# Attention and mixture-of-experts layer: the work between the two phases is placed anew, ten record loads change queue, and the second weights are loaded one expert at a time

## The chip, the cores and the metric

The kernel runs on one core of a Trainium2 chip. The engines of the core run programs of their own and meet by semaphores: TensorE (PE in the profile) multiplies matrices, VectorE (DVE), ScalarE (ACT) and GpSimd (POOL) work elementwise, SyncE (SP) issues transfers. The metric is the device time of one execution in microseconds (us). Before the change it was 968.32 us in the median of three runs (965.58 to 971.52).

## What is computed

32 blocks of 128 tokens with 256 features. First cross-attention with 16 heads and an unusual score, then a feed-forward layer with 8 experts, of which each token takes 2:

```python
x = x + attention(layernorm(x), ctx) @ Wo + bo
# feed-forward: t tokens, 8 experts, H = 1024
logits = einsum('btd,de->bte', layernorm(x), Wr)
w, idx = top_k(softmax(logits), 2);  w = w / sum(w)
h = gelu(einsum('btd,edh->ebth', x, W1) + b1)
y = einsum('ebth,ehd->ebtd', h, W2) + b2
out = x + einsum('ebtd,bte->btd', y, dispatch)
```

## The kernel before

The first phase walks over 16 pairs of token blocks (`NP` = 16). In it attention is computed, the tokens are routed, and each token's normalised features, its shares and its number are written as a record of 265 words into the table `xrec` in HBM, at a row of its expert (`scatter`, indirect DMAs of GpSimd). On the side the weights are turned into two halves of float16; the first weights stay in SBUF (`w1s`), the second go to HBM (`w2s`) by `store_w2`.

The second phase takes 71 slots (`NSLOT`) of 128 records, all of one expert each. Slot s has these steps:

- `load_records(s)`: SP loads 128 records into `rb`, of which there are ten (`U`). Slot s + 10 can be loaded when `add(s)` has landed.
- `turn_records(s)` on TensorE turns them, `take_records(s)` on VectorE copies them to `xt`.
- `first_product(s)`: 48 matmuls on TensorE into one of two pairs of banks. The weights of the expert are at an address in a register, since the expert of a slot is known at run time only (`expert_of` loads it).
- `gelu(s)` on ScalarE, eight activations; `split_hidden(s)` on VectorE makes two halves of float16.
- `second_product(s)`: 24 matmuls on TensorE.
- `weigh(s)` on VectorE: scale, bias, share; into one of two `yw`.
- `add(s)` on GpSimd: an indirect DMA that adds the 128 rows to `out`. It waits for the landing of `add(s-1)`.

Each engine's program is written out by hand in order. In the loop over s, TensorE runs turn(s+3), first(s+2), second(s); ScalarE runs gelu(s); VectorE runs take(s+3), split(s+2), weigh(s). TensorE's turn(s+1) waits for take(s), because there is one bank for it; `weigh(s)` waits for the landing of `add(s-2)`, because there are two `yw`.

The first twenty slots (`SOON`) are laid out from the counts of the first 24 blocks, so that the second phase can begin before the last pairs are routed. The rest of the work for the last pair (`project_out`, `heads_back`, `turn_on`, `residual`, `turn_y`, `record_high`, `record_low`, `logits`, `choose`, `counts`, `ranks`, `shares`, `positions`, `scatter`, `last_tables`) is interleaved with the first slots. `last_tables` lays out slots 20 to 70. `record_low(b)` on GpSimd waits for `record_high(b)` on ScalarE; both halves stand in GpSimd's program ahead of `add(0)`.

On SP, the lines around the change are: load records 0 to 8, store the last of the second weights, load all eight experts' second weights (`w2s_sb`, 1 MB each) behind one another without a wait, tell TensorE expert by expert that they are there (`w2_ready`), and load records 9 to 19.

## Time and profile before

| | |
|---|---|
| median of three runs | 968.32 us |
| the profiled execution | 970.74 us |
| its span, first to last instruction | 968.9 us |
| mean granted TensorE clock | 0.977 of full |
| PE busy | 898.1 us (93%) |
| DVE busy | 697.2 us (72%) |
| ACT busy | 634.5 us (65%) |
| POOL busy | 415.5 us (43%) |

The times of the rows are microseconds from the start of the span. A timeline row gives start, length, engine, line, operation, output and inputs, the number of instructions merged into it, and in brackets how long the engine was idle before it and which instruction ended that. "issue" means that the profile shows nothing that was waited for.

### The profile page before, as it was taken

To read this page: it belongs to the slowest core of one execution; us is meant where nothing else is said; L and a number is where in the kernel's file an instruction comes from. 1 tells how busy PE (TensorE), PEld (TensorE's weight loads), DVE (VectorE), ACT (ScalarE), POOL (GpSimd) and SP (SyncE) were. 2 spreads that over 40 slices of the span, in tenths; PEclk is the share of its full clock that TensorE was granted. 3 is DMA by queue.
4 is the path that set the end of the run, shared out by engine and by line. 5 is a ranking of instruction groups with operands and counts; after the bars stand their busy time and mean duration, and the time that the engine had idled before them with its cause. 6 is when DMAs were issued, how large, how long until landed. Compare 5 with 4: busy or idle time off the path is not lost.

```text
span 968.9 us, 30634 instructions
## 1 busy us (share of the span) xinstructions
PE 898.1 (93%) x10701; PEld 789.8 (82%) x10701; DVE 697.2 (72%) x1833; ACT 634.5 (65%) x1236; POOL 415.5 (43%) x540
## 2 busy tenths in 40 slices
PE   3999999998999999989899699899999999999994
PEld 2788887787877877878777589799999999999993
DVE  7677888777987887779768577766666666666662
ACT  3688887787877877878857356455555455554551
POOL 6344456538546565385253532623222232222322
PEclk9799999999999999999979799999999999999998
DMA  5222122314132333253044773443333233332222
GB/s 150 70 72 89 41 83 80 112 41 128 57 99 76 126 123 103 92 171 111 20 139 134 275 273 52 85 93 52 51 52 51 47 52 52 52 51 48 46 30 22
DMA packets 61892, 84.82 MB, mean 88 GB/s; under 512 B 9872, under 2 KB 55312, under 8 KB 59568
## 3 DMA queue, kind: packets, MB, share of 16 engines
q1 hardware_dynamic: 47504, 64.26, 21.0%
q0 software_dynamic: 13296, 18.00, 11.1%
q8 instruction: 91, 1.49, 0.6%
q10 hardware_dynamic: 944, 0.60, 0.2%
q14 instruction: 57, 0.47, 0.2%
HBM read 49.86 MB, written 31.92 MB: 84 GB/s over the span
## 4 chain that ended last, share of the span: by engine, by line
PE 74%; issue 7%; DVE 6%; ACT 6%; POOL 3%; another core or an unknown queue 1%; DMA 1%; DVEq 0%; POOLq 0%; ACTq 0%
PE s_ps L711 10%; PE u_ps L711 10%; PE pv_ps L729 9%; PE gen L729 9%; PE gen L502 5%; PE gen L495 5%; PE s_ps L485 5%; PE u_ps L473 3%; PE pv_ps L519 2%; PE gen L544 2%; ACT pt L827 2%; PE gen L415 2%; PE gen L680 2%; PE gen L418 2%; PE gen L422 1%
## 5 line engine op out<-in xcount | busy, mean ns | idle before, releaser
L1567 POOL DMA_INDIRECT out<-yw,rb x71 | 110.3, 1553 | 269.4 <-DVE yw L1392 253.4
L928 ACT ACTIVATE h<-s_ps,b1t,inv 128x128 f32<-128x128 f32 x288 | 107.8, 457 | 89.6 <-PE s_ps L711 79.3
L928 ACT ACTIVATE h<-u_ps,b1t,inv 128x128 f32<-128x128 f32 x280 | 104.7, 459 | 87.4 <-PE u_ps L711 86.4
L1375 DVE TENSOR_SCALAR hs<-h,hsc 128x512 f16<-128x512 f32 x142 | 69.7, 491 | 120.4 <-ACT h L928 102.0
L827 ACT ACTIVATE pt<-gen,escale 128x512 f32<-128x512 f32 x128 | 86.8, 686 | 50.4 <-PE gen L502 34.5
L1377 DVE SCALAR_TENSOR_TENSOR hs<-h,hsc,hs 128x512 f16<-128x512 f32 x142 | 106.7, 751 | 5.1
L711 PE MATMUL s_ps<-xt,w1s 128*128 128x128 f16 x1728 | 104.8, 220 | 2.2 <-issue 2.2
L1517 POOL DMA_INDIRECT xrec<-rec,idx x64 | 77.8, 1215 | 60.9 <-DVE idx L1229 44.7
L711 PE MATMUL u_ps<-xt,w1s 128*128 128x128 f16 x1680 | 102.5, 220 | 0.9 <-issue 0.9
L711 PEld LDWEIGHTS s_ps<-xt,w1s 128*128 x1728 | 99.8, 99 | 2.8 <-issue 2.3
L729 PE MATMUL pv_ps<-w2s_sb,hs 128*128 x864 | 100.5, 272 | 0.5 <-issue 0.5
L711 PEld LDWEIGHTS u_ps<-xt,w1s 128*128 x1680 | 97.2, 99 | 2.0 <-issue 1.5
L1124 DVE SCALAR_TENSOR_TENSOR tw<-th,s_ps 128x1024 f32<-128x1024 f32 x64 | 77.9, 1217 | 27.2 <-PE s_ps L485 21.9
L729 PE MATMUL gen<-w2s_sb,hs 128*128 x840 | 97.4, 273 | 0.0
L729 PEld LDWEIGHTS pv_ps<-w2s_sb,hs 128*128 128x128 f16 x864 | 82.5, 98 | 11.0 <-issue 1.5
L495 PE MATMUL gen<-idf,tw 128*128 128x128 f32 x512 | 79.5, 278 | 10.7 <-DVE wcl L1283 7.9
L502 PE MATMUL gen<-negb,mhl 128*128 128x128 bf16 x1024 | 79.2, 220 | 9.7 <-POOL mhl L1488 9.3
L729 PEld LDWEIGHTS gen<-w2s_sb,hs 128*128 128x128 f16 x840 | 80.9, 98 | 8.8
L1130 DVE TENSOR_REDUCE tm<-tw 128x8 f32<-128x1024 f32 x64 | 78.1, 1220 | 2.2
L817 ACT ACTIVATE th<-u_ps 128x1024 f32<-128x1024 f32 x64 | 65.6, 1026 | 20.5 <-PE u_ps L473 20.3
L502 PEld LDWEIGHTS gen<-negb,mhl 128*128 128x128 bf16 x1024 | 67.9, 99 | 13.6 <-POOL mhl L1488 11.6
L485 PE MATMUL s_ps<-kt,qt 32*128 32x128 f32 x1024 | 75.6, 286 | 0.9 <-DVE tw L1124 0.9
(251 smaller groups left out, 1741.8 us busy)
## 6 DMA issues: line engine op xcount, KB each, us to landing
wl<-L_ffn_W SPq DMA_DIRECT2D x16, 1024.0 KB
rb<-xrec SPq DMA_DIRECT2D x71, 132.5 KB
w2s<-wst SPq DMA_DIRECT2D x8, 1024.0 KB
w2s_sb<-w2s SPq DMA_DIRECT2D x8, 1024.0 KB, 20.4
xin<-x SPq DMA_DIRECT2D x32, 128.0 KB, 3.5
cin<-ctx SPq DMA_DIRECT2D x32, 128.0 KB, 2.1
xres<-x SPq DMA_DIRECT2D x32, 128.0 KB
out<-x SPq DMA_DIRECT2D x30, 128.0 KB, 2.0
```

Source lines behind the costliest of these rows:

```text
L485: ins = pe.matmul(s_ps[:, i, j * P:(j + 1) * P], qt[b][rws, j // 2, :], kt[b][rws, j // 2, j % 2, :], start=True, stop=True)
L495: pe.matmul(g[:, j * P:(j + 1) * P], tw[h][:, i, j, :], idf[:, :], is_transpose=True, start=(j == 0), stop=False)
L502: ins = pe.matmul(g[:, j * P:(j + 1) * P], m, negb[:, :], start=False, stop=(j == 3 and part == 1))
L711: ins = pe.matmul(hbank[n % HBANKS][:, o:o + SLOT], w, xt[s % 2][:, xp, k, :], start=(t == 0), stop=(t == len(terms) - 1))
L729: ins = pe.matmul(y, hs[s % 3][:, hp, m, :], w, start=(m == 0 and t == 0), stop=(m == HC - 1 and t == 2))
L827: act.activation(pt[n % 2][:, i, :], turn(f"ex{n}{i}", p)[:, :], ACT.Exp, scale=escale[:, :]).then_inc(sig(f"ex{n}{i}"), 1)
L928: ins = act.activation(h32[n % HBANKS][:, m % HB, :], hbank[n % HBANKS][:, o:o + SLOT], ACT.Gelu, scale=inv1[:, bass.ds(ex, 1)].bitcast(F3 ...
L1124: dve.scalar_tensor_tensor(tw[h][:, :, :, :].rearrange("p i j k -> p (i j k)"), th[h][:, :], -1.0, s_ps[:, :, :].rearrange("p i k -> p (i ...
L1130: dve.tensor_reduce(tm[h][:, :], tw[h][:, :, :, :].rearrange("p i j k -> p (i j) k"), AX.X, ALU.max).then_inc(sig(f"tm{n}"), 1)
L1377: dve.scalar_tensor_tensor(lo, h, scale, hi, ALU.mult, ALU.subtract).then_inc(sig("lo"), 1)
L1517: pool.indirect_dma_start(xrec_d[:, :], bass.IndirectOffsetOnAxis(ap=idx[:, i, t:t + 1], axis=0), rec[m % 2][:, t, :], None).then_inc(sig( ...
L1567: pool.indirect_dma_start(out[:, :], bass.IndirectOffsetOnAxis(ap=rb[j][:, D + NE:D + NE + 1], axis=0), yw[s % 2][:, :], None, compute_op= ...
```

## The change

**SP.** `b2s`, now placed first in the memory of the second phase, is loaded ahead of the records. Ten record loads follow instead of nine, then the second weights: each expert's load begins when the one before has landed. The store of the last second weights comes ahead of expert 2, and a wait for all stores ahead of expert 5. Records 10 to 19 are no longer loaded by SP.

**GpSimd.** It loads records 10 to 19 itself, each between the landing of `add(s-1)` and the issue of `add(s)`, s from 1 to 10. The scatters of the last pair move from slots 5 to 8 to slots 9 to 12.

**TensorE, ScalarE, VectorE.** The first slots begin ahead of the rest of the last pair, and that work is spread over later slots. Addresses for `first_product` are computed ahead for the first slots too. ScalarE loads its gelu table before the first slot. VectorE's `weight_low` of the last pair and most of the scale steps (`hidden_scales`, without `inv1`) come later. From slot 60 on (`SHORT`) TensorE runs first(s+1), second(s).

```diff
+    gelu_one = alloc(ctx, "gelu_one", [P, 1], F32)
...
+            for b in range(2):
+                sp.wait_ge(*at(f"v{b}", NP))
+            sp.dma_start(b2s[:, :, :], b2.partition_broadcast(P)).then_inc(sig("ldb2"), 16)
             sp.wait_ge(*at("soon", 1))
             sp.wait_ge(*dma("scat", 4 * (SOON_PAIR + 1)))
-            for b in range(2):
-                sp.wait_ge(*at(f"v{b}", NP))
-            for s in range(U - 1):
+            for s in range(U):
                 load_records(s)
-            store_w2(NP - 1)
             sp.wait_ge(*at("pv3", NP))
-            for e in range(NE - 1):
+            for e in range(NE):
+                if e == 2:
+                    store_w2(NP - 1)
+                if e == W2_SOON:
+                    sp.wait_ge(*dma("stw", NE))
                 load_w2(e)
-                if e == 0:
-                    sp.dma_start(b2s[:, :, :], b2.partition_broadcast(P)).then_inc(sig("ldb2"), 16)
-            sp.wait_ge(*dma("stw", NE))
-            load_w2(NE - 1)
-            for e in range(NE):
                 sp.wait_ge(*dma(f"ldw2_{e}", 1))
                 sp.sem_inc(sig("w2_ready"), 1)
-            for s in range(U - 1, SOON):
-                load_records(s)
...
-                pe.wait_ge(*dma(f"ldrec{s % U}", s // U + 1))
+                if U <= s < SOON:
+                    pe.wait_ge(*dma(f"ldsoon{s % 5}", 1 if s < U + 5 else 2))
+                else:
+                    pe.wait_ge(*dma(f"ldrec{s % U}", s // U if s >= SOON else 1))
...
-            def first_product(s, ex):
+            def first_product(s, ex, ahead=()):
...
+                        for address in itertools.islice(ahead, 2 * DC):
+                            pe.to_reg(address)
...
+            experts = [expert_of(pe, 0)]
+            for address in first_addresses(experts[0]):
+                pe.to_reg(address)
+            turn_records(0)
             project_out(0, NP - 1)
+            experts.append(expert_of(pe, 1))
+            turn_records(1)
+            first_product(0, experts[0], first_addresses(experts[1]))
             heads_back(1, NP - 1)
-            for s in range(3):
-                turn_records(s)
-            experts = [expert_of(pe, s) for s in range(3)]
-            first_product(0, experts[0])
+            turn_records(2)
+            experts.append(expert_of(pe, 2))
+            first_product(1, experts[1], first_addresses(experts[2]))
             turn_on(1, NP - 1)
-            first_product(1, experts[1])
-            project_out(1, NP - 1)
-            turn_y(0, NP - 1)
             for s in range(NSLOT):
                 if s + 3 < NSLOT:
                     turn_records(s + 3)
-                if s + 2 < NSLOT:
-                    first_product(s + 2, experts[2])
+                if s + 2 < SHORT:
+                    first_product(s + 2, experts[2], second_addresses(experts[0]) if s == 0 else ())
+                elif SHORT - 2 < s < NSLOT - 1:
+                    first_product(s + 1, experts[1], second_addresses(experts[0]))
                 if s == 0:
+                    project_out(1, NP - 1)
+                if s == 1:
+                    turn_y(0, NP - 1)
+                if s == 2:
                     logits(0, NP - 1)
+                if s == 3:
                     turn_y(1, NP - 1)
-                if s == 1:
+                if s == 4:
                     logits(1, NP - 1)
-                if s == 4:
+                if s == 7:
                     ranks(NP - 1)
                 if s + 3 < NSLOT:
                     experts.append(expert_of(pe, s + 3))
-                later = second_addresses(experts[1]) if s + 1 < NSLOT else ()
-                second_product(s, experts[0], itertools.chain(later, first_addresses(experts[3]) if s + 3 < NSLOT else ()))
+                if s + 3 < SHORT:
+                    ahead = itertools.chain(second_addresses(experts[1]), first_addresses(experts[3]))
+                elif s + 3 == SHORT:
+                    ahead = second_addresses(experts[1])
+                elif s + 2 < NSLOT:
+                    ahead = first_addresses(experts[2])
+                else:
+                    ahead = ()
+                second_product(s, experts[0], ahead)
...
+            act.activation(gelu_one[:, :], mhalf[:, :], ACT.Gelu)
...
-                    act.wait_ge(*at("scales", 1))
+                    act.wait_ge(*at("inv1", 1))
...
             for s in range(NSLOT):
                 gelu(s)
-                if s == 0:
+                if s == 1:
                     o_turned(1, NP - 1)
-                if s == 1:
+                if s == 2:
                     store_x1(0, NP - 1)
                     record_high(0, NP - 1)
-                if s == 2:
+                if s == 5:
+                    store_x1(1, NP - 1)
                     record_high(1, NP - 1)
-                    store_x1(1, NP - 1)
-                if s == 5:
+                if s == 7:
                     route_exp(NP - 1)
...
-                if 0 <= it - 1 < NP:
+                if 0 <= it - 1 < NP - 1:
...
+            take_records(0)
+            dve.tensor_scalar(inv1[:, :], k1[:, :], 25.0, float(ONE), ALU.subtract, ALU.mult).then_inc(sig("inv1"), 1)
+            take_records(1)
+            hidden_scales()
+            experts = [expert_of(dve, s) for s in range(2)]
             residual(0, NP - 1)
-            heads_back(1, NP - 1)
-            take_records(0)
-            take_records(1)
-            experts = [expert_of(dve, s) for s in range(2)]
             split_hidden(0, experts[0])
             take_records(2)
-            residual(1, NP - 1)
+            heads_back(1, NP - 1)
             split_hidden(1, experts[1])
             for s in range(NSLOT):
                 if s + 3 < NSLOT:
                     take_records(s + 3)
-                if s == 0:
-                    logits(0, NP - 1)
                 if s + 2 < NSLOT:
                     experts.append(expert_of(dve, s + 2))
+                if s + 2 < SHORT:
                     split_hidden(s + 2, experts[2])
+                elif SHORT - 2 < s < NSLOT - 1:
+                    split_hidden(s + 1, experts[1])
+                if s == 0:
+                    weight_low(NP - 1)
                 if s == 1:
+                    residual(1, NP - 1)
+                if s == 2:
+                    logits(0, NP - 1)
+                if s == 4:
                     logits(1, NP - 1)
                 weigh(s, experts[0])
                 experts.pop(0)
-                if s == 1:
+                if s == 5:
                     choose(NP - 1)
-                if s == 2:
+                if s == 6:
                     counts(NP - 1)
-                if s == 5:
+                if s == 8:
                     shares(NP - 1)
-                if s == 6:
+                if s == 9:
                     positions(NP - 1)
-                if s == 7:
+                if s == 10:
                     last_tables()
...
+            def load_records(s):
+                j = s % U
+                if s >= U + 5:
+                    pool.wait_ge(*dma(f"ldsoon{s % 5}", 1))
+                row = pool.value_load(slot_row[0:1, s:s + 1], min_val=0, max_val=NE * REGION)
+                pool.dma_start(rb[j][:, :], xrec_d[bass.ds(row, SLOT), :]).then_inc(sig(f"ldsoon{s % 5}"), 16)
...
                 if s:
                     pool.wait_ge(*dma(f"add{(s - 1) % U}", (s - 1) // U + 1))
+                    if s - 1 + U < SOON:
+                        load_records(s - 1 + U)
...
-                if 5 <= s < 9:
+                if 9 <= s < 13:
                     for i in range(2):
-                        scatter(s - 5, i, NP - 1)
+                        scatter(s - 9, i, NP - 1)
...
+    W2_SOON = 5
+    SHORT = 60
...
+        b2s = alloc(f, "b2s", [P, NE, D], F32)
```

`hidden_scales` holds the eight scale steps that stood ahead of the second phase, without the one for `inv1`.

Three places show how rows move. The first is TensorE at the start of the second phase, before (L541 and L544 are `project_out`, L680 `turn_records`, L269 `expert_of`, L711 `first_product`):

```order
L541 MATMUL gen<-bop,ones_b 128x256 [waits act_exp]
L544 MATMUL gen<-wo_sb,ot 128x256 [waits ote]
L544 MATMUL gen<-wo_sb,ot 128x256
L527 MATMUL gen<-idf,osb 128x128 [waits osb,ote]
L527 MATMUL gen<-idf,osb 128x128 x3
L680 MATMUL gen<-id,rb 128x128 [waits dve_route,ldrec0]
L680 MATMUL gen<-id,rb 128x128 x3
...
L269 TENSOR_LOAD slot_e
L269 ISA x2
L711 ISA [waits dve_max,xte]
L711 MATMUL s_ps<-xt,w1s 128x128 x2
L711 REGISTER_ALU
```

and now (L681 is `turn_records`, L270 `expert_of`, L740 the addresses ahead, L712 and L715 `first_product` with the addresses of the next slot):

```order
L270 TENSOR_LOAD slot_e [waits soon]
L270 ISA x2
L740 ISA x6
L681 MATMUL gen<-id,rb 128x128 [waits dve_route,ldrec0]
L681 MATMUL gen<-id,rb 128x128 x3
L539 MATMUL gen<-bop,ones_b 128x256 [waits act_exp]
L542 MATMUL gen<-wo_sb,ot 128x256 [waits ote]
...
L712 MATMUL s_ps<-xt,w1s 128x128 [waits dve_max,xte]
L712 MATMUL s_ps<-xt,w1s 128x128 x5
L715 ISA
L712 MATMUL s_ps<-xt,w1s 128x128 x6
```

The turn of slot 0 stands ahead of `project_out`, and the register instruction that stood before nearly every matmul has become one group for each six.

The second place is ScalarE. Before, the record's high half of block 1 (L847) and the store (L935) stood behind the gelu of slot 2:

```order
L928 ISA
L928 ACTIVATE h_1<-s_ps,b1t,inv 128x128
L847 ACTIVATE rec<-xn 128x256 [waits y1,scat]
L851 ACTIVATE xn2t<-gen 128x256 [waits lg,xu1]
L935 DMA out<-x 128x256 [waits dve_second1]
L269 TENSOR_LOAD slot_e
L269 ISA x2
```

Now they stand behind the gelu of slot 5 (L952), L959 being the store and L868 the high half:

```order
L952 ISA
L952 ACTIVATE h_3<-u_ps,b1t,inv 128x128
L959 DMA out<-x 128x256 [waits dve_second1]
L868 ACTIVATE rec<-xn 128x256 [waits y1,scat]
L872 ACTIVATE xn2t<-gen 128x256 [waits lg,xu1]
L270 TENSOR_LOAD slot_e
L270 ISA x2
```

The third is GpSimd behind the two `record_low`, before:

```order
L1493 TENSOR_TENSOR rec<-xn,rec 128x256 [waits rh0]
L1493 TENSOR_TENSOR rec<-xn,rec 128x256 [waits rh1]
L1567 DMA out<-yw,rb 4224x256 [waits stx1,stx0,yw]
L1567 DMA out<-yw,rb 4224x256 [waits add0,yw]
L1567 DMA out<-yw,rb 4224x256 [waits add1,yw]
```

and now (L1607 is `add`, L1591 and L1592 `load_records`):

```order
L1524 TENSOR_TENSOR rec<-xn,rec 128x256 [waits rh0]
L1524 TENSOR_TENSOR rec<-xn,rec 128x256 [waits rh1]
L1607 DMA out<-yw,rb 4224x256 [waits stx1,stx0,yw]
L1591 TENSOR_LOAD slot_row [waits add0,yw]
L1591 ISA x2
L1592 ISA
L1592 DMA rb<-xrec 128x265
L1607 DMA out<-yw,rb 4224x256
L1591 TENSOR_LOAD slot_row [waits add1,yw]
```

A register load and a plain DMA have come between one add and the next.

## Rows read from the trace of the kernel before

**Rows 1.** Windows view: stretch, its length, busy us (instructions) by engine, clock, DMA.
```profile
core 0: us, PE busy (x) PEld busy (x) DVE busy (x) ACT busy (x) POOL busy (x), PEclk, DMA share, GB/s
616.00:621.00 5.00, 4.09 (x47) 3.53 (x45) 3.67 (x8) 1.97 (x6) 2.66 (x3) 0.70 0.53 113
624.00:900.00 276.00, 276.00 (x3801) 262.43 (x3800) 177.52 (x350) 150.14 (x400) 78.09 (x51) 1.00 0.33 55
```

**Rows 2.** Timeline of TensorE at the start of the second phase.
```profile
538.44 0.28 PE L541 MATMUL gen<-bop,ones_b 96*128 96x256 bf16 x1
...
539.86 0.39 PE L680 MATMUL gen<-id,rb 128*128 128x128 f16 x4
546.74 0.59 PE L680 MATMUL gen<-id,rb 128*128 128x128 f16 x4 [6.50 <-DVE xt L1362]
...
550.51 4.10 PE L711 MATMUL s_ps<-xt,w1s 128*128 128x128 f16 x48 [1.99 <-issue]
...
554.74 3.94 PE L711 MATMUL u_ps<-xt,w1s 128*128 128x128 f16 x48
```

**Rows 3.** Timeline of TensorE, slots 7 and 12 and 13.
```profile
585.52 0.39 PE L680 MATMUL gen<-id,rb 128*128 128x128 f16 x4
585.75 2.84 PE L711 MATMUL s_ps<-xt,w1s 128*128 128x128 f16 x48
...
615.69 0.38 PE L680 MATMUL gen<-id,rb 128*128 128x128 f16 x4 [1.93 <-DVE xt L1362]
...
624.04 0.39 PE L680 MATMUL gen<-id,rb 128*128 128x128 f16 x4
```

**Rows 4.** Timeline of VectorE.
```profile
538.72 2.35 DVE L1277 SCALAR_TENSOR_TENSOR wst<-wl,wsc,wst 128x2048 f16<-128x2048 f32 x1
540.98 0.16 DVE L960 TENSOR_SCALAR kb<-b1ss 128x8 int32<-128x8 int32 x1
...
544.28 0.42 DVE L1154 TENSOR_TENSOR x<-gen,xres 128x256 f32<-128x256 f32 x1
...
545.49 0.25 DVE L1137 RECIPROCAL rz<-gen 128x16 f32<-128x16 f32 x1
...
556.40 0.49 DVE L1375 TENSOR_SCALAR hs<-h,hsc 128x512 f16<-128x512 f32 x1 [8.62 <-ACT h L928]
...
558.87 0.41 DVE L1362 COPY xt<-gen 128x512 f16<-128x512 f16 x1
...
568.82 0.48 DVE L1386 SCALAR_TENSOR_TENSOR yb<-pv_ps,inv,b2s 128x256 f32<-128x256 f32 x1 [0.92 <-PE pv_ps L729]
...
569.73 0.42 DVE L1362 COPY xt<-gen 128x512 f16<-128x512 f16 x1
...
608.75 0.48 DVE L1386 SCALAR_TENSOR_TENSOR yb<-gen,inv,b2s 128x256 f32<-128x256 f32 x1
```

**Rows 5.** Timeline of ScalarE.
```profile
565.01 0.35 ACTq L935 DMA_DIRECT2D out<-x  x1
565.30 0.43 ACT L847 ACTIVATE rec<-xn 128x256 f16<-128x256 f32 x1
...
576.37 2.90 ACT L928 ACTIVATE h<-s_ps,b1t,inv 128x128 f32<-128x128 f32 x8 [3.03 <-issue]
```

**Rows 6.** Timeline of GpSimd: a scatter, a low half, the last three adds.
```profile
542.35 0.96 POOL L1517 DMA_INDIRECT xrec<-rec,idx  x1 [0.31 <-issue]
...
565.81 1.02 POOL L1493 TENSOR_TENSOR rec<-xn,rec 128x256 f16<-128x256 f32 x1 [1.61 <-DMA out<-x]
...
951.83 1.55 POOL L1567 DMA_INDIRECT out<-yw,rb  x1 [3.92 <-DVE yw L1392]
956.94 1.54 POOL L1567 DMA_INDIRECT out<-yw,rb  x1 [3.56 <-DVE yw L1392]
961.44 1.55 POOL L1567 DMA_INDIRECT out<-yw,rb  x1 [2.95 <-DMA out<-yw,rb]
```

**Rows 7.** SP's timeline with the record loads; landing of the eight loads of L363.
```profile
528.31 9.58 SPq L360 DMA_DIRECT2D rb<-xrec  x9
...
DMA to landing us min/median/max: 14.2/20.4/26.4
```

18 lines of the change are left out of this document (8 added, 10 removed).

## Prediction

> **What bounds the kernel now.** I read the windows view first. From 624 to 900 us TensorE is busy all the time at full clock, 3801 matmuls, and one slot has 76 of them (4 turns of the records, 48 of `first_product`, 24 of `second_product`), so a slot takes 276 / 50 = 5.52 us [rows 1]. I write turn(s), fp(s), sp(s), take(s), split(s), weigh(s), add(s) for the steps of slot s. The change leaves those matmuls alone; only where TensorE stands still can it gain or lose. The timeline of TensorE shows three such places. At the entry TensorE ends the attention work at about 540.3, waits 6.50 us for VectorE's `xt`, then 1.99 us for nothing but its own sequencer ("issue"), and starts fp(0) at 550.51 [rows 2]. Around 615 turn(12) waits 1.93 us for `last_tables`, and from turn(12) to turn(13) 8.35 us pass instead of 5.52 [rows 3], with a granted clock of 0.70 from 616 to 621 [rows 1]. At the end three adds follow one another on GpSimd at 951.83, 956.94 and 961.44, each held by the landing of the last: 5.1 and 4.5 us apart [rows 6].
>
> Times below are on the clock of the trace of before; LAND(s) is the landing of add(s).
>
> **Entry, a gain.** `weight_low` leaves the path (2.35 us [rows 4]), most of the scale steps come behind take(1), and addresses are computed ahead: fp(1) took 3.94 us for what 2.84 us do later, at a full clock, with a register instruction before most of its matmuls; that is 1.1 us for each of three slots [rows 2, 3]. Worked through: values end at 538.4; one value load costs 1.99 / 3 = 0.66, and I give the eight register rows 0.5: turn(0) at 539.6. take(0), `project_out(0)` (with `heads_back` 1.4 us in the trace, I take 1.0) and a second value load put fp(0) at 541.8, its end at 544.5. VectorE: take(1) by 542.3; scales 540.98 to 544.28 are 3.3 us, less 0.7 for `inv1`, now ahead: 544.9; two value loads 1.3; `residual(0)` 1.2; split(0) 2.5 (556.40 to 558.87): 549.9, take(2) 550.3, `heads_back` 0.7 [rows 4]. TensorE's `turn_on` waits for that: fp(2) at 551.5. From here a slot is 5.5 plus what stands between: `project_out(1)` 1.0, `turn_y` 0.3, `logits` 0.5. fp(5) starts at 569.9, and TensorE would be free for turn(7) at 575.5. Before it came at 585.52 [rows 3]: 10.0 us ahead. The gelu table load runs beside idle time. Bounds: 1 us earlier if the value loads cost half, 3 later if ScalarE's wait in `record_high(0)` for `turn_y(0)` reaches TensorE.
>
> **The hold, a new wait.** `record_high(1)` now stands behind gelu(5). GpSimd has `record_low(1)`, which needs it, ahead of add(0); weigh(2) waits for LAND(0); and behind weigh(2) on VectorE is take(6), for which turn(7) waits. gelu(5) ends at 569.9 + 1.35 (half of fp) + 0.2 + 2.90 = 574.4; DMA issue and copy 0.72 [rows 5]; `record_low` 1.02; add(0) starts at 576.3; landing seen 4.6 later (between 4.5 and 5.1 [rows 6]): LAND(0) = 580.9. weigh and take are 1.4, so turn(7) comes at 582.3: 6.8 us lost of the 10.0, and 3.2 left. Before, nobody waits there.
>
> **The chain of adds.** Records 10 to 19 leave SP's queue for GpSimd's, each between LAND(s-1) and add(s), for s = 1 to 10. SP needs 9.58 us for nine such loads, (9.58 - 0.34) / 8 = 1.155 apart, of which 0.34 is the DMA instruction: 0.8 for the value load and registers [rows 7]. GpSimd's DMA issue is nearest to the scatter's 0.96; the add's 1.55 and SP's 0.34 are the ends [rows 6, 7]. So an add takes 4.5 + 0.8 + 0.96 = 6.3 us in this stretch; from below 4.5 + 0.8 + 0.34 = 5.6, from above 5.1 + 0.8 + 1.55 + 0.3 = 7.75. That is more than 5.52, and the hold has used up the slack: weigh(s) waits for LAND(s-2). LAND(8) = 580.9 + 8 x 6.3 = 631.3. `choose`, `counts` and `ranks`, now at slots 5 to 7, fit into the 0.8 us per slot that TensorE gets back as idle time, with the chain still ahead at slot 10.
>
> Behind weigh(10) stands `last_tables`. In the trace from the start of such a weigh to the turn are 615.69 - 608.75 = 6.9 us [rows 3, 4]. So turn(15) comes at 638.2. Before it is at 624.04 + 2 x 5.52 = 635.1. Loss 3.1. TensorE has then been idle about 6 us (1.93 us ahead of the low clock in the trace); I charge the same 8.35 - 5.52 = 2.8 us again [rows 3], between 0 and 4.
>
> The Trainium skill ("DMA: Bandwidth & Descriptors", "Latency and other measured facts") gives a floor of about 600 ns for `tensor_load`; SP's 0.8 us agrees with it. By the same page, "Issuing engine by pattern", a plain load belongs on SP; it gives about 1 us to the first byte from GpSimd and 0.6 us from SP. With only 0.6 + 0.96 the chain would have a period of 6.1 us and the time would be 1.9 us lower. No row here shows a plain load from GpSimd.
>
> **Other loads.** `load_w2(0)` is issued at about 539.6, behind ten record loads at 1.155 us and `b2s`, and sp(0) comes at 555. Before, a megabyte among nine took 14.2 to 26.4 us [rows 7]; even 14.2 is enough, and alone it should be less. Expert 2's load waits behind `weight_low` (about 560), but experts come in order, some six slots each (the 24 blocks counted by then give 24 x 128 x 2 / 8 = 768 rows to each of eight), so nobody asks for it before 590. Cost 0. Slots from 20 on need the eight late scatters (behind adds 9 to 12, done about 655); turn(20) is past 665: 10 us of cover, cost 0.
>
> **Tail.** From slot 60 the first product runs one slot ahead instead of two. sp(68) moves ahead of fp(70), 2.7 us, so add(68) is at 949.1, add(69) 5.1 later, add(70) at 958.7 instead of 961.44: gain 2.7. TensorE's own end does not move. Between 0 and 2.9.
>
> **Sum.** 3.1 + 2.8 - 2.7 = 3.2 us slower. The profiled execution lasted 970.74 us, its span 968.9; the median of the three runs is 968.32, 2.4 below it. On the median: **971.5 us**. About 1% is what a measurement of this kernel can tell from no change, so I forecast no change.
>
> **The rivals.**
> - *Slower: the load's cost on GpSimd is that of an add.* With 1.55 us of descriptor work and some of the load's packets before the add's, the period is 7.6: 971.5 + 8 x 1.3 = 982 us. It decides (over 978) from a period of 7.1. For it: this is the same queue, and GpSimd's indirect DMAs take 0.96 to 1.55. Against: a plain load has no index per row. 0.22.
> - *The load is cheap,* period 5.6: 971.5 - 8 x 0.7 = 966 us. For it: SP's 0.34. Against: no DMA of GpSimd's in the trace is under 0.96. 0.16.
> - *Faster: the hold is not paid.* If add(0) lands while VectorE is busy anyway, 6.8 us come back; without the hold the adds have some 5 us of slack, so with a cheap load the chain (another 5.6 us) and 3 us of the bubble at turn(15) go too: about 956 us. One of them alone is not 1%. Against it stands the row order of three engines. 0.13.
> - *Another wait at the entry* (`turn_y(0)`, the second weights) takes 3 to 6 us more than I charged; since the chain starts from it, all of it stays: 975 to 978. 0.09.
> - *The forecast,* 968 to 977 with periods between 5.9 and 7.0: 0.40, the largest share.
>
> **Range and chances.** From 963, where half of the hold and a cheap load meet, to 982, the slow rival. Faster by over 1% (under 958.6): 0.13; within 1%: 0.63; slower by over 1% (over 978.0): 0.24.
>
> **What would show each step.** fp(0) near 542 and no "issue" wait before it (entry). The first add of GpSimd some 2 us behind the end of gelu(5), and TensorE idle 6 to 7 us before turn(7), released by `xt` (hold). Adds 1 to 10 spaced 6.3 us, with a VectorE wait for "DMA out" before `yw` (chain). A gap of 5 to 6 us before turn(15) with a granted clock near one half behind it (`last_tables`). The last add 2.7 us closer to TensorE's end (tail). I am wrong if the first add is issued before 570, if adds 1 to 10 keep 5.5 us, or if TensorE waits for `w2_ready`.

## The result, and the profile after the change

The changed kernel takes 985.88 us in the median of four runs (983.95 to 987.14), the kernel before 967.91 us in four runs that include one beside it. The ratio is 1.0181, with a 95% interval of 1.0144 to 1.0217. It is slower by 1.8%, where 971.5 us and no change were forecast, and above the range's upper end of 982.

| | before | after |
|---|---|---|
| median | 967.91 us | 985.88 us |
| the profiled execution | 970.74 us | 986.65 us |
| its span | 968.9 us | 985.0 us |
| mean granted clock | 0.977 | 0.969 |
| the last attention matmul ends | 538.4 us | 536.2 us |
| from there to turn(7) | 47.1 us | 53.8 us |
| from there to turn(17) | 107.7 us | 125.9 us |
| from turn(17) to the span's end | 322.8 us | 322.9 us |

The end of the last attention matmul differs from profile to profile (533.4 to 539.1 us in those on chips of this speed), so I count from there. The whole loss, 18.2 us, lies between it and turn(17). Behind turn(17) nothing is lost and nothing won.

TensorE's timeline of the changed kernel (start us, us, engine, line, operation, output and inputs, count, and the idle time before it with what ended it):

```profile
535.33 0.94 PE L517 MATMUL pv_ps<-pt,vz 128*32 128x128 f32 x16
...
539.14 2.84 PE L712 MATMUL s_ps<-xt,w1s 128*128 128x128 f16 x48
...
549.78 0.66 PE L532 MATMUL gen<-idf,on 128*128 128x128 f32 x2 [3.54 <-DVE on L1166]
...
550.66 4.82 PE L712 MATMUL s_ps<-xt,w1s 128*128 128x128 f16 x48
...
568.32 4.50 PE L732 MATMUL gen<-w2s_sb,hs 128*128 x24 [6.11 <-SPq L381]
...
590.04 0.59 PE L681 MATMUL gen<-id,rb 128*128 128x128 f16 x4 [5.54 <-DVE xt L1376]
590.42 5.33 PE L712 MATMUL s_ps<-xt,w1s 128*128 128x128 f16 x48
...
619.88 0.19 PE L562 MATMUL gen<-hot,lstrict 128*128 128x32 bf16 x1 [3.23 <-DVE acc_cnt L1216]
...
620.74 5.28 PE L732 MATMUL gen<-w2s_sb,hs 128*128 x24 [0.64 <-issue]
```

There are four waits of over 3 us, and behind each the next product runs for 4.5 to 5.3 us: 4.82 and 5.33 for a first product that takes 2.84 undisturbed, 4.50 and 5.28 for a second product that takes 2.78. It pays another 1.7 to 2.5 us. The waits are at `turn_on` (before fp(2)), at sp(1), at turn(7), and at the ranks before sp(7). A shorter wait, 2.06 us at turn(10), is followed by a first product of 4.47 us. The first and the third wait were forecast with what is waited for, `heads_back` and the hold; the second and the fourth were not, and of the low clock behind any of the four nothing was charged.

GpSimd's timeline of the changed kernel, from the release of the first add:

```profile
583.97 0.64 POOL L1524 TENSOR_TENSOR rec<-xn,rec 128x256 f16<-128x256 f32 x1 [12.26 <-ACT rec L868]
584.77 1.67 POOL L1607 DMA_INDIRECT out<-yw,rb  x1 [0.17 <-issue]
590.62 0.63 POOL L1592 DMA_DIRECT2D rb<-xrec  x1 [4.18 <-issue]
591.56 1.72 POOL L1607 DMA_INDIRECT out<-yw,rb  x1 [0.30 <-issue]
596.81 0.60 POOL L1592 DMA_DIRECT2D rb<-xrec  x1 [3.53 <-DVE yw L1406]
597.72 1.62 POOL L1607 DMA_INDIRECT out<-yw,rb  x1 [0.30 <-issue]
```

This is the hold and the chain: the first add leaves 1.3 us behind the ScalarE copy of 583.46 that it was held for, and add(1) to add(10) stand 6.22 us apart in the mean (591.56 to 647.55 in nine steps, the single ones 5.92 to 7.10).

### The profile page after: what moved, and what is told of

It reads as the page before. It is cut to its first block, busy times and chain, and to the rows that moved or that the text cites. A ratio compares the mean times of both kernels' runs of the same rounds, so it can differ in the third digit from the quotient of the medians.

```text
span 985.0 us, 30587 instructions
## 1 busy us (share of the span) xinstructions
PE 904.3 (92%) x10701; PEld 795.3 (81%) x10701; DVE 693.9 (70%) x1833; ACT 633.6 (64%) x1237; POOL 420.5 (43%) x550
## 4 chain that ended last, share of the span: by engine, by line
PE 69%; issue 10%; ACT 6%; DVE 5%; POOL 4%; DMA 2%; another core or an unknown queue 1%; POOLq 0%; ACTq 0%; DVEq 0%
PE gen L732 9%; PE s_ps L712 8%; PE pv_ps L732 8%; PE u_ps L712 8%; PE gen L500 5%; PE gen L493 5%; PE s_ps L483 5%; PE u_ps L471 2%; PE pv_ps L517 2%; PE gen L542 2%; ACT pt L848 2%; DMA out<-yw,rb 2%; PE gen L413 2%; PE gen L416 2%; PE gen L681 1%
## 5 line engine op out<-in xcount | busy, mean ns | idle before, releaser
L1607 POOL DMA_INDIRECT out<-yw,rb x71 | 110.5, 1557 | 230.3 <-DVE yw L1406 211.6
L952 ACT ACTIVATE h<-s_ps,b1t,inv 128x128 f32<-128x128 f32 x288 | 106.6, 461 | 111.2 <-PE s_ps L712 110.6
L952 ACT ACTIVATE h<-u_ps,b1t,inv 128x128 f32<-128x128 f32 x280 | 104.3, 461 | 91.3 <-PE u_ps L712 88.5
L732 PE MATMUL gen<-w2s_sb,hs 128*128 x840 | 102.0, 280 | 7.2 <-SPq L381 6.1
L712 PE MATMUL s_ps<-xt,w1s 128*128 128x128 f16 x1728 | 107.1, 224 | 0.2 <-issue 0.2
L712 PEld LDWEIGHTS s_ps<-xt,w1s 128*128 x1728 | 102.7, 101 | 0.3 <-issue 0.3
L712 PE MATMUL u_ps<-xt,w1s 128*128 128x128 f16 x1680 | 101.5, 221 | 0.6 <-issue 0.6
L712 PEld LDWEIGHTS u_ps<-xt,w1s 128*128 x1680 | 97.0, 99 | 0.9 <-issue 0.9
```

The source lines that it names most:

```text
L712: ins = pe.matmul(hbank[n % HBANKS][:, o:o + SLOT], w, xt[s % 2][:, xp, k, :], start=(t == 0), stop=(t == len(terms) - 1))
L732: ins = pe.matmul(y, hs[s % 3][:, hp, m, :], w, start=(m == 0 and t == 0), stop=(m == HC - 1 and t == 2))
L952: ins = act.activation(h32[n % HBANKS][:, m % HB, :], hbank[n % HBANKS][:, o:o + SLOT], ACT.Gelu, scale=inv1[:, bass.ds(ex, 1)].bitcast(F3 ...
L1607: pool.indirect_dma_start(out[:, :], bass.IndirectOffsetOnAxis(ap=rb[j][:, D + NE:D + NE + 1], axis=0), yw[s % 2][:, :], None, compute_op= ...
```

## The experiments

All times count from the end of the last attention matmul of the kernel's own profile. "To the end" is the span less that point. The ratio is to the kernel before, run beside it.

| kernel | median us | ratio [95%] | turn(7) | turn(17) | to the end |
|---|---|---|---|---|---|
| before | 967.91 | 1 | 47.1 | 107.7 | 430.5 |
| after | 985.88 | 1.0181 [1.0144, 1.0217] | 53.8 | 125.9 | 448.8 |
| r1_residual | 983.59 | 1.0172 [1.0137, 1.0207] | 49.7 | 120.4 | 443.5 |
| r2_store5 | 984.21 | 1.0190 [1.0154, 1.0225] | 52.2 | 123.1 | 446.4 |
| r3_hold | 980.48 | 1.0135 [1.0100, 1.0170] | 48.1 | 118.0 | 440.4 |
| r4_sploads | 983.33 | 1.0177 [1.0140, 1.0214] | 53.0 | 121.6 | 443.9 |
| t1_ranks | 981.91 | 1.0154 [1.0137, 1.0172] | 53.7 | 120.0 | 443.4 |
| t2_four | 965.79 | 0.9987 [0.9970, 1.0004] | 41.1 | 105.5 | 427.5 |
| t4_pool_loads | 970.65 | 1.0007 [0.9980, 1.0034] | 40.8 | 109.9 | 435.1 |
| t5_all | 961.43 | 0.9914 [0.9880, 0.9948] | 40.8 | 99.4 | 421.6 |
| t6_all_entry | 959.13 | 0.9896 [0.9874, 0.9919] | 40.6 | 99.3 | 421.9 |
| d1_residual_late | 966.37 | 1.0003 [0.9980, 1.0025] | 47.9 | 106.1 | 428.2 |
| d2_hold_back | 966.39 | 0.9998 [0.9980, 1.0015] | 46.2 | 106.3 | 428.2 |
| d3_ranks_early | 967.04 | 0.9990 [0.9973, 1.0007] | 41.0 | 106.5 | 428.3 |
| d4_loads_gpsimd | 970.55 | 1.0032 [1.0006, 1.0058] | 41.1 | 106.9 | 430.2 |
| s3_before_short | 964.71 | 0.9982 [0.9964, 1.0000] | 47.2 | 105.9 | 426.1 |
| s4_before_serial | 967.08 | 1.0001 [0.9987, 1.0015] | 47.6 | 105.3 | 427.7 |

Two more ran beside each other on a faster chip, where the kernel before takes 956.34 us: d5_serial_w2 955.19 us, 0.9988 [0.9967, 1.0009], and t7_all_again (t5_all once more) 948.03 us, 0.9922 [0.9896, 0.9949]. Their turn(17) comes at 104.4 and 98.5. The kernels of the table ran on several chips, on which the kernel before took 966.19 to 969.32 us, so between kernels the ratios compare better than the medians.

### One repair at a time

**The residual ahead of split(3).** The profile names a SyncE semaphore, L381, for the wait of sp(1); but slot 1 is of expert 0, whose weights sp(0) had used 12 us before. What stands directly ahead of it in time is VectorE:

```profile
565.32 0.49 DVE L1389 TENSOR_SCALAR hs<-h,hsc 128x512 f16<-128x512 f32 x1 [3.37 <-ACT h L952]
...
567.13 0.75 DVE L1391 SCALAR_TENSOR_TENSOR hs<-h,hsc,hs 128x512 f16<-128x512 f32 x1
567.80 0.42 DVE L1178 TENSOR_TENSOR x<-gen,xres 128x256 f32<-128x256 f32 x1
```

The last row is `residual(1)`. It reads the bank of `project_out(1)`, which is sp(1)'s result bank, and it ends at 568.22; sp(1) starts at 568.32. The change put it behind split(3), which waits for gelu(3), and gelu(3) stands on ScalarE behind `record_high(0)`, whose copy waited 4.81 us for `turn_y(0)`:

```profile
562.25 0.38 ACT L872 ACTIVATE xn2t<-gen 128x256 f32<-128x256 f32 x1 [4.81 <-PE gen L549]
563.67 2.90 ACT L952 ACTIVATE h<-u_ps,b1t,inv 128x128 f32<-128x128 f32 x8 [1.04 <-issue]
```

```diff
+                if s == 1:
+                    residual(1, NP - 1)
                 if s + 2 < SHORT:
                     split_hidden(s + 2, experts[2])
...
-                if s == 1:
-                    residual(1, NP - 1)
```

> The changed kernel with one step moved: VectorE's residual of the last block stands ahead of split(3), not behind it. Theory (the bank): sp(1) writes the bank that the output projection of the last block filled, and waits 6.1 us for VectorE to read it there; the gap before sp(1) goes (568.3 to about 562) and with it the 1.7 us that sp(1) ran slower at the low clock; both stay, since the chain of adds starts from gelu(5): 985.9 less 7 to 8, about 978. Rival (the second weights, which the profile names as what ended that wait): sp(1) still waits 6 us, 985.9 unchanged.

The wait of sp(1) shrank to 0.75 us and turn(6) stands at 35.2 instead of 42.4:

```profile
565.46 2.78 PE L732 MATMUL gen<-w2s_sb,hs 128*128 x24 [0.75 <-issue]
```

But turn(7) came only at 49.7: TensorE waited 8.55 us there for VectorE, which waited 12.5 us for the landing of an add. Of 7.2 us at turn(6), 5.5 were left at turn(17), and the median shows 2.3, where 7 to 8 were expected. The rival on the wait's cause has its own run:

```diff
-                if e == 2:
-                    store_w2(NP - 1)
                 if e == W2_SOON:
+                    store_w2(NP - 1)
                     sp.wait_ge(*dma("stw", NE))
```

> The changed kernel with the store of the last second weights put ahead of expert 5's load instead of expert 2's, so that the loads of experts 2 to 4 do not wait for VectorE's late half of those weights. Rival (sp(1) waits for second weights): they land at about 560, the wait of 6.1 us goes, about 978. Theory (the bank): sp(1) needs expert 0 only, the wait stays, 985.9 within 1.5 us.

The wait at sp(1) stayed, at 5.43 us, though SyncE had issued the loads of experts 0 to 4 by 558.1:

```profile
564.14 4.98 PE L731 MATMUL gen<-w2s_sb,hs 128*128 x24 [5.43 <-issue]
```

So it was not the second weights. In all three kernels sp(1) starts 0.10 us behind the end of `residual(1)`: 568.32 behind 568.22 in the changed kernel, 565.46 behind 565.36 in r1_residual, 564.14 behind 564.04 in r2_store5. The bank is shown by the pair of runs, and the name in the row was of a semaphore that had been met. The median of r2_store5 is 1.7 us lower and its ratio 0.09% higher, which tells nothing.

**The hold.** The high half of `record_high(1)` behind gelu(3); its second copy, now `copy_turned(1)`, stays behind gelu(5):

```diff
...
+                if s == 3:
+                    record_high(1, NP - 1)
                 if s == 5:
                     store_x1(1, NP - 1)
-                    record_high(1, NP - 1)
+                    copy_turned(1, NP - 1)
```

> The changed kernel with the high half of the last block's record made behind gelu(3); the store and the copy of the turned block stay behind gelu(5). Theory (the hold): GpSimd's low half runs at about 572, add(0) lands at 577 instead of 589, TensorE's wait of 5.5 us before turn(7) and the slow fp(6) (5.3 us for 2.8) go, and the adds are no longer behind: about 985.9 less 10, between 6 and 13. Rival (the late first add only uses slack, the entry sets the end): unchanged.

add(0) left at 574.61 and turn(7) waited for nothing. This is the largest gain of the single repairs: 7.9 us at turn(17), of which the median shows 5.4, just under the 6 to 13 expected.

**The record loads on SyncE again**, behind the second weights:

```diff
+            for s in range(U, SOON):
+                load_records(s)
...
-                    if s - 1 + U < SOON:
-                        load_records(s - 1 + U)
```

> The changed kernel with records 10 to 19 loaded by SP again, behind the second weights. The hold stays. Theory (the chain of adds): adds come 4.6 us apart until they have caught up, then 5.5 us, instead of 6.2; choose and ranks find VectorE in time; about 985.9 less 8, between 5 and 10. Rival (GpSimd's loads run inside waits that are there anyway): unchanged within 1.5 us.

The first six adds closed up to 4.92, 4.97, 5.59, 4.48 and 4.81 us. With the hold and the residual still in front, the time moved by 2.6 us in the median, 4.3 at turn(17): more than the rival's 1.5, less than the 5 to 10 of the theory.

**The ranks one slot later** on TensorE:

```diff
-                if s == 7:
+                if s == 8:
                     ranks(NP - 1)
```

> The changed kernel with ranks on TensorE one slot later (s == 8 for 7), nothing else. In all five traces with the new placement 13 us pass from turn(10) to turn(11) instead of 5.5: TensorE waits 3 to 5 us for VectorE's counts, which is late because ScalarE sat in route_exp, and then runs sp(7) at the low clock. Theory (several chains run side by side, so that one repair shows only down to the next): the wait and the low clock behind it go, but the adds of GpSimd, still 6.1 us apart since the late first one, hold turn(15) at about 111 us behind the attention's end instead of 114: 2 to 4 us faster than the changed kernel. Rival (the losses are independent and add): 8 us faster.

5.9 us less at turn(17), 4.0 in the median, the upper end of what the theory expected.

### Two parts put into the kernel before

```diff
-                if s + 2 < NSLOT:
+                if s + 2 < SHORT:
                     first_product(s + 2, experts[2])
+                elif SHORT - 2 < s < NSLOT - 1:
+                    first_product(s + 1, experts[1], second_addresses(experts[0]))
```

> The kernel before with only the end changed: from slot 60 first product one slot ahead instead of two, with its addresses. Prediction's term: the last add 2.7 us earlier, TensorE's own end where it was, so 965.5 for 968.2. Rival: the span's end does not follow the last add (behind the last add 9.9 us passed in the changed kernel, 7.5 before), so no gain.

```diff
-            for e in range(NE - 1):
+            for e in range(NE):
+                if e == NE - 1:
+                    sp.wait_ge(*dma("stw", NE))
                 load_w2(e)
...
+                sp.wait_ge(*dma(f"ldw2_{e}", 1))
+                sp.sem_inc(sig("w2_ready"), 1)
```

> The kernel before with only the second weights loaded one expert at a time, each at the landing of the last. Prediction's term: 0, within 1.5 us of before. Rival (TensorE waits for w2_ready, as the profile of the changed kernel names it): a wait of some us in front of sp(0) or sp(1), 3 to 6 us slower.

The first product one slot ahead from slot 60 (s3) brings a gain at the edge of what the times can show, 0.18% (interval 0 to 0.36%). The profile shows it plainly: the last add starts 3.91 us behind TensorE's end (955.24 behind 951.33) instead of 6.35 (961.44 behind 955.09), and from turn(17) to the end 320.2 us pass instead of 322.8. That is the tail's 2.7 us, within 0.1.

The second weights one by one (s4) cost nothing in the kernel before. Both profiles reach turn(17) 2 us earlier than that of the kernel before: from turn(12) to turn(13) 8.35 us pass in the profile on which the forecast rests, with a granted clock of 0.70 from 616 to 621, but 6.58 us in s3 and 5.64 in s4, with a clock of 1.00 there. So the 2.8 us that I took for the low clock is one execution's value.

### All together, and each put back

t2_four holds the four repairs (residual, hold, ranks, loads on SyncE):

> The changed kernel with four steps put right at once: residual of the last block ahead of split(3), its high half behind gelu(3), records 10 to 19 loaded by SP, ranks at slot 8. Theory: no chain is left to take over; turn(17) comes 102 to 105 us behind the attention's end instead of 125.9 (before: 107.7), and the tail keeps its 2.7 us: 15 to 22 us faster than the changed kernel and 0 to 1% faster than before. Rival (the repairs overlap with something not yet seen): not more than the 4.4 us that the hold alone gave, still over 1% slower than before.

It gives back 20 us in the median and 1.94% in the ratio. The single repairs (residual, hold, loads, ranks) gave 2.3, 5.4, 2.6 and 4.0 us in their medians, and only 0.09, 0.46, 0.04 and 0.27% in the ratios to the kernel before on their own chips, each uncertain by some 0.35%. A new wait stands at turn(10), because record 10 is now behind eight second weights loaded one after another:

```profile
600.76 0.40 PE L680 MATMUL gen<-id,rb 128*128 128x128 f16 x4 [4.10 <-DMA rb<-xrec]
```

Two ways around it. t4_pool_loads has t2_four's repairs but for that of the loads. Its expectation says that `choose` and `counts` move too; the edit moves `ranks` alone, as in t2_four:

> The changed kernel with three repairs: the residual of slot 1 stands ahead of split(3) on VectorE, the hold at turn(7) is gone, and choose, counts and ranks stand one slot later (ranks at slot 8). The records' loads stay on GpSimd. Theory: the record wait of 4.1 us that TensorE showed at turn(10) in t2_four is gone, since no record load stands behind a second-weights load on SyncE any more, but the adds stay 6.1 to 6.3 us apart and GpSimd's last DRAIN is 5.6 us where t2_four had 4.8: 962 to 966 us. Rival (the loads of records on GpSimd are the main cost): above 972 us.

> All of t4_pool_loads, and route_exp one slot later, the records of slots 10 to 19 on SyncE, and the second weights of experts 0 to 4 queued together ahead of the store, 5 to 7 one after another. Theory: no record waits behind a serial load, the waits at turn(10) to turn(12) are under 1 us, 958 to 963 us. Rival (the wait moves to another buffer at the same place): 964 to 968 us, as t2_four.

The theory of t4 missed: leaving the loads on GpSimd gave 970.65 us, 5 us over it and just under the rival. TensorE waits over 2 us at three turns instead of one, turn(9), turn(10) and turn(15), for a VectorE that had waited 5.61, 2.57 and 0.94 us for the landing of an add and then had its own work to do, at turn(10) that of `choose` and at turn(15) that of `last_tables`:

```profile
590.16 0.38 PE L681 MATMUL gen<-id,rb 128*128 128x128 f16 x4 [2.19 <-DVE xt L1382]
...
599.26 0.59 PE L681 MATMUL gen<-id,rb 128*128 128x128 f16 x4 [3.41 <-DVE xt L1382]
...
633.02 0.59 PE L681 MATMUL gen<-id,rb 128*128 128x128 f16 x4 [3.09 <-DVE xt L1382]
```

t5_all queues the second weights of experts 0 to 4 together, stores, and then queues 5 to 7, so that within each of the two groups no load waits for the landing of the one before. It also has the records on SyncE and `route_exp` at slot 8 (both not shown here):

```diff
-            for e in range(NE):
-                if e == 2:
-                    store_w2(NP - 1)
-                if e == W2_SOON:
+            for first, last in ((0, W2_SOON), (W2_SOON, NE)):
+                if first:
+                    store_w2(NP - 1)
                     sp.wait_ge(*dma("stw", NE))
-                load_w2(e)
-                sp.wait_ge(*dma(f"ldw2_{e}", 1))
-                sp.sem_inc(sig("w2_ready"), 1)
+                for e in range(first, last):
+                    load_w2(e)
...
```

It beats both kernels: 961.43 us, 0.9914, and 0.9922 when run again. From turn(3) to turn(14) its turns are 5.5 to 8.6 us apart, with no bubble until the one of `last_tables` (1.64 us):

```profile
552.56 0.66 PE L535 MATMUL gen<-idf,on 128*128 128x128 f32 x2 [1.92 <-issue]
...
553.44 4.77 PE L712 MATMUL s_ps<-xt,w1s 128*128 128x128 f16 x48
...
626.46 0.38 PE L681 MATMUL gen<-id,rb 128*128 128x128 f16 x4 [1.64 <-DVE xt L1382]
```

Then each part was put back alone, by taking its diff above out of t5_all (d3 has both `ranks` and `route_exp` at slot 7 again).

> t5_all with the residual of slot 1 back behind split(3) on VectorE, as the change has it. Theory (each part of the change that stands at slots 1 to 10 costs by itself once the others are gone): sp(1) waits some 6 us on its bank and runs 1.7 us longer at the low clock, so 966 to 970 us. Rival (something later takes the time up, as it did in r1_residual, where this repair alone gave back 2 us): 961 to 963 us, as t5_all.

> t5_all with record_high(1) back at slot 5 on ScalarE, so that record_low on GpSimd holds add(0), as the change has it. Theory: turn(7) waits for the landing of add(0), 5 to 7 us and some 2 us of low clock behind it: 966 to 970 us. Rival (the hold is taken up): 961 to 963 us.

> t5_all with route_exp on ScalarE and counts and ranks on TensorE back at slot 7. Theory: a wait of 3 to 5 us at ranks(15) and the low clock behind it: 964 to 968 us. Rival: 961 to 963 us.

> t5_all with the loads of records 10 to 19 back on GpSimd, each between two adds. Theory (t4_pool_loads against t5_all): the adds stand 6.2 us apart, more than the 5.5 us of a slot, weigh waits for their landings and TensorE for VectorE, and the last DRAIN is 5.6 instead of 4.8 us: 967 to 971 us. Rival (the 9 us between t4_pool_loads and t5_all come from the second weights or route_exp): 961 to 964 us.

> t5_all with the second weights one after another again, the store ahead of expert 2 and the wait for all stores ahead of expert 5, as the change has them; the records stay on SyncE, behind all of these. Theory: the record of slot 10 comes late, TensorE waits about 4 us at turn(10) as in t2_four, 964 to 967 us. Rival (route_exp one slot later is what made t5_all faster than t2_four): 961 to 963 us.

Each came out as its theory said, the first four with medians at 966 to 971 us. d5_serial_w2 ran on the faster chip; its ratio of 0.9988 stands 0.66% above that of t7_all_again, and it keeps `route_exp` at slot 8, so it was not this step that made t5_all faster than t2_four. TensorE's timelines show the wait of each; here those of d1, d2, d3 and d5:

```profile
565.32 4.52 PE L732 MATMUL gen<-w2s_sb,hs 128*128 x24 [6.02 <-issue]
```

```profile
580.58 0.58 PE L681 MATMUL gen<-id,rb 128*128 128x128 f16 x4 [5.13 <-DVE xt L1376]
```

```profile
604.71 0.19 PE L565 MATMUL gen<-hot,lstrict 128*128 128x32 bf16 x1 [4.59 <-DVE acc_cnt L1222]
```

```profile
589.97 0.40 PE L680 MATMUL gen<-id,rb 128*128 128x128 f16 x4 [4.00 <-DMA rb<-xrec]
```

In d1 the same wait is put down to "issue": the name of a releaser can change where the cause doesn't. In d3 it begins on ScalarE, whose `route_exp` stands ahead of gelu(8) and waits for twelve small VectorE instructions of `choose`, with a change of activation table on either side:

```profile
590.81 1.28 ACT L881 ACT_TABLE_LOAD   x1
596.36 0.20 ACT L881 ACTIVATE rs_e<-rs_d 128x4 f32<-128x4 f32 x1 [4.26 <-DVE rs_d L1212]
597.07 1.28 ACT L956 ACT_TABLE_LOAD   x1 [0.51 <-issue]
598.36 2.90 ACT L956 ACTIVATE h<-s_ps,b1t,inv 128x128 f32<-128x128 f32 x8
```

The prices at turn(17) against t5_all are 106.1 - 99.4 = 6.7 us for the residual, 6.9 for the hold, 7.1 for the ranks, 7.5 for the loads on GpSimd; the medians give 4.9, 5.0, 5.6 and 9.1, and the ratios 0.89, 0.84, 0.76 and 1.18%. For the serial second weights the pair on the faster chip differs by 5.9 us at turn(17), 7.2 in the median and 0.66% in the ratio. Together that is 34 us at turn(17), 32 in the medians and 4.3% in the ratios, for what costs 125.9 - 99.4 = 26.5 us at turn(17), 24.5 in the medians and 2.7% in the ratios of after and t5_all. By all three measures, then, the losses lie partly beside each other: with one gone the next shows, as turn(7) does in r1_residual.

The single repairs don't decide this. Their ratios add to 0.9% and their medians to 14 us, where the four together give 1.9% and 20 us. But at turn(17) of the profiles they add to 5.5 + 7.9 + 4.3 + 5.9 = 23.6 us, more than the 20.4 of the four together. Each profile is one execution.

> t5_all once more, beside d5_serial_w2 on the same chip, so that the parts put back can be compared with it: 960 to 963 us, 0.7 to 1.1% under the kernel before.

The ratio is 0.78% under the kernel before, as expected; the time of 948.03 us is lower than the 960 to 963 because everything is on that chip (956.34 us for the kernel before).

One try at the wait before `turn_on`, by taking `heads_back(1)` ahead of take(2) and split(0) on VectorE:

```diff
             residual(0, NP - 1)
-            split_hidden(0, experts[0])
-            take_records(2)
             heads_back(1, NP - 1)
+            take_records(2)
+            split_hidden(0, experts[0])
```

> t5_all, and on VectorE at the entry the order residual(0), heads_back(1), take(2), split(0), so that TensorE does not wait 3.6 us for heads_back ahead of turn_on, and fp(2), which took 4.8 us at the low clock behind that wait, takes 2.8 to 3.9. Theory: 3 to 5 us less than t5_all, 955 to 959 us. Rival: the 3.6 us go to another wait before turn(3), and nothing is gained within 1 us.

Neither the theory (3 to 5 us) nor the rival (none within 1 us) is decided. The median is 2.3 us lower (958.90 to 960.39, against 959.10 to 964.67 of t5_all) and the ratio 0.18%, less than the intervals of the two; counted from the end of attention t5_all takes 421.6 us and t6_all_entry 421.9; the first product behind the wait still takes 5.00 us. The turns to 17 agree within 0.6 us, so the profiles don't show a gain in the stretch that was edited. Whether the 2.3 us are real, and where they come from, stays open. At 0.9896 its ratio is the lowest of the study.

### GpSimd's last instruction

The kernel before, with the last pair's scatters four slots later:

```diff
-                if 5 <= s < 9:
+                if 9 <= s < 13:
...
```

> The kernel before with GpSimd's scatters of the last pair moved from slots 5 to 8 to slots 9 to 12. Theory A: GpSimd's last DRAIN grows with how late its last transfers or scatters stand, so it goes from 3.05 us to 4.8 us or more. Theory B: it goes by the number of transfers that GpSimd itself has issued, and stays at 3.05 us. The time within 0.5% of the kernel before by either.

The rows of L1600 in the kernel before, of the same line in s5_before_scatter, and of L1642 in the changed kernel (duration in ns: least, median, largest; start in us). s5_before_scatter took 967.64 us in its one run, beside 969.32 of the kernel before:

```profile
L1600 POOLq DRAIN  x1: 3053/3053/3053, 965.6 to 965.6; - x1
```

```profile
L1600 POOLq DRAIN  x1: 4809/4809/4809, 960.7 to 960.7; - x1
```

```profile
L1642 POOLq DRAIN  x1: 5589/5589/5589, 979.2 to 979.2; - x1
```

Theory A held: the four slots by which the last scatters move add 1.76 us. Over all profiles the three with the scatters at slots 5 to 8 have 3053 ns, the ten with late scatters and records on SyncE have 4809, and the seven that also load ten records on GpSimd have 5589. So the loads add another 0.78 us; d4_loads_gpsimd and t5_all differ in them alone. From the start of the last add to the span's end 7.46 us pass in the kernel before, 9.07 in s5_before_scatter and 9.91 in the changed kernel. Why the DRAIN has these lengths isn't shown.

## Why the prediction was wrong

On the clock of the kernel before (2.2 us are added to what the changed kernel's trace shows), step by step:

- **Entry, fp(0) at 541.8.** Measured 541.4, right. **fp(2) at 551.5**: 552.9, 1.4 late. It then took 4.82 us instead of 2.84. The order of events was right, the low clock behind the 3.5 us wait was not charged.
- **Entry, "fp(5) starts at 569.9".** This is the step that failed. turn(6), directly ahead of it, was to come at 569.7 and came at 580.8, 11.1 us late. t5_all has it at 573.5 (35.1 from the end of attention), so 3.8 us are the entry and its low clock, and 7.3 are the wait of sp(1) for `residual(1)`. I had counted every TensorE step, but not the owner of sp(1)'s result bank, and so this wait stood in the sum at nothing. The row's name for it, the second weights, was one of my signs of being wrong; r1 and r2 show that it was not them. The sentence "3 later if ScalarE's wait in `record_high(0)` for `turn_y(0)` reaches TensorE" named the wait at which it began, at less than half of its price, and not the way by which it reached TensorE.
- **Hold.** The mechanism was right in each link (ScalarE's copy, `record_low`, add(0), weigh(2), take(6), turn(7)). The size was not quite: of the 6.8 us TensorE waited 5.54, and in d2 turn(7) is 5.4 us behind that of t5_all. That d2 prices the hold at 6.9 us at turn(17) is partly luck, since 1.3 of these are the low clock (fp(6) 4.16 us for 2.84), which wasn't charged; in the changed kernel fp(6) took 5.33 us. Since the hold began from a late turn(6), turn(7) was 9.9 us late (592.2 for 582.3).
- **Chain of adds.** Period 6.22 us in the mean against 6.3, right: the load's issue takes 0.60 to 0.63 us with 0.30 behind it, together 0.90 to 0.93 for the 0.96 that I took. The Trainium skill ("DMA: Bandwidth & Descriptors", "Issuing engine by pattern") would keep a plain load on SyncE; the 7.5 us of d4 agree with it here.
- **"`choose`, `counts` and `ranks` ... fit into the 0.8 us per slot".** Wrong. They were weighed as TensorE work, but it is a round through VectorE, ScalarE and VectorE again that stands in front of gelu(8). From turn(10) to turn(11) 13.9 us pass instead of 5.5. In the changed kernel part of this lies beside the chain: t1_ranks gives back 5.9 us at turn(17) (4.0 in the median), while d3, with `route_exp` early too, costs 7.1 (5.6) where nothing else holds.
- **turn(15) at 638.2.** Came at 652.2, 14.0 late: 9.9 from turn(7), 4.1 more between the two. Of the 4.1 the low clock behind turn(7) and the ranks account for more than enough; how they divide against the chain's slack is not shown.
- **Low clock behind `last_tables`, 2.8 us.** There was none. The wait before turn(15) was 1.66 us and not about 6, fp(14) behind it took 2.84 us, and the granted clock from 645 to 664 was 1.00. From turn(15) to turn(17) 12.1 us still pass instead of 11.0, with short pauses in the rows for which the profile shows no wait. 13.8 was forecast, so 1.7 were charged too much, and 12.3 us are late at turn(17).
- **Other loads, cost 0.** Right for the kernel before (s4, ratio 1.0001), and for expert 2. They have a price of 6 to 7 us once everything else is repaired and the records are behind them on SyncE.
- **Tail, gain 2.7.** The last add came 3.65 us behind TensorE's end (971.44 to 975.09), where it was 6.35 in the kernel before: 2.7 nearer, as worked out. But behind the last add 9.9 us pass instead of 7.5, of which 5.59 - 3.05 = 2.54 are the longer DRAIN. The net is about nothing: 322.9 us from turn(17) to the end against 322.8. In s3, where the DRAIN kept its length, the gain is there.

TensorE behind `last_tables` in the changed kernel, and the window behind turn(15) (granted clock third from the end):

```profile
650.05 0.38 PE L681 MATMUL gen<-id,rb 128*128 128x128 f16 x4 [1.66 <-issue]
650.27 2.84 PE L712 MATMUL s_ps<-xt,w1s 128*128 128x128 f16 x48
...
662.15 0.39 PE L681 MATMUL gen<-id,rb 128*128 128x128 f16 x4
```

```profile
650.00:656.00 6.00, 5.86 (x80) 5.46 (x81) 4.92 (x10) 2.90 (x8) 3.18 (x3) 1.00 0.63 165
```

In the terms of the sum, counted from the end of attention: the loss up to turn(15), 3.1 us in the forecast, measured 17.2; the 2.8 behind it measured 1.1; and the gain of 2.7 at the end measured nothing.

All of it together: 12.3 late at turn(17) and 2.8 lost at the tail are 15.1; the first phase ended 2.2 us earlier, and the changed kernel's profiled execution was 0.8 above its median where 2.4 was assumed. 15.1 - 2.2 + 1.6 = 14.5, against the 985.88 - 971.5 = 14.4 us by which the forecast missed.

The rivals: "slower" had a period of 7.6 us as its mechanism, which no add showed. The nearest was "another wait at the entry", with `turn_y(0)` and 3 to 6 us, 975 to 978 in all. It was the right place at half the size or less (11.1 us late at turn(6)), with a chance of 0.09.

## What to carry over

- When work of one phase is spread over the slots of the next, list for each moved step the banks and buffers that it releases and who takes them next, and walk that engine's order up to it. The bank of `residual(1)`, a step of 0.42 us, cost 7 us.
- A step that crosses engines (`choose` to `route_exp` to `counts` to `ranks`) has to be priced on its longest way, not on the engine that ends it. And a stall of TensorE can cost more than its own length: the four over 3 us in the changed kernel had another 1.7 to 2.5 us behind them at the low clock.
- Where several waits stand side by side, repair everything and then put the parts back one by one. Here the four single repairs added to 14 us in the medians and 23.6 at turn(17), where the four together gave 20, and their ratios moved by 0.04 to 0.46% with an uncertainty of 0.35; the parts put back alone moved it by 0.66 to 1.18%, each with one wait to see.

## What the runs showed of the hardware

- GpSimd's last DRAIN had one exact length for each arrangement of its transfers: 3053, 4809 or 5589 ns. It grew when the scatters stood later, and again when GpSimd issued ten plain loads. In the changed kernel it is 2.54 us longer than before.
- A plain load issued by GpSimd takes 0.60 to 0.63 us there, and an add that has one ahead of it stands 6.2 us behind the last, where the last three adds of the kernel before stand 4.5 to 5.1 us apart. In r4_sploads the first six adds were 4.48 to 5.59 us apart.
- The first products behind waits of 3.54 and 5.54 us took 4.82 and 5.33 us for 2.84. The windows of the changed kernel (PEclk is the third number from the end) show the granted clock near one half of full, the lower of the two levels (1.2 GHz) for most of each stretch:

```profile
550.00:556.00 6.00, 6.00 (x58) 5.88 (x58) 3.10 (x7) 3.58 (x11) 0.96 (x1) 0.60 0.13 42
590.00:596.00 6.00, 5.96 (x56) 5.99 (x57) 3.09 (x7) 1.62 (x5) 2.36 (x2) 0.52 0.62 197
```

- Not every wait of TensorE was followed by the low clock, and its length alone doesn't tell. A wait of 2.06 us (changed kernel, turn(10)) and one of 2.55 (t1_ranks, turn(11)) had a first product of 4.47 us behind them; waits of 3.04 (t1_ranks, turn(10)) and 3.68 us (d4_loads_gpsimd, turn(15)) had one of 2.84, at a granted clock of 1.00. The rows of d4_loads_gpsimd:

```profile
634.42 0.38 PE L682 MATMUL gen<-id,rb 128*128 128x128 f16 x4 [3.68 <-DVE xt L1383]
634.64 2.84 PE L713 MATMUL s_ps<-xt,w1s 128*128 128x128 f16 x48
```
